# A fused decoder layer with top-k cross-attention: two row normalisations and a residual add change engines, and two stages change the order of their instructions

## The reference

```python
x = x + attn(layernorm(x))        # 4 branches x 16 heads, RMS norm and rope on q, banded masks, null values
x = x + xattn(layernorm(x), ctx)  # 16 heads; softmax over the 32 largest of 722 scores, times the values
x = x + ffn(layernorm(x))         # fft, a sparse complex weight, inverse fft: one real 512 x 512 matrix

def layernorm(x): return (x - mean(x)) / sqrt(var(x) + 1e-5)      # over the last axis
```

## Time and profile before

| | us |
|---|---|
| median of three runs | 2447.41 (2444.17 to 2450.51) |
| the profiled execution's own time | 2448.53 |
| its span | 2446.7 |

### The profile page before, as it was taken

One profiled execution on the slowest core, in us unless ns is written; L12 is line 12 of the kernel. 1 busy time (PEld: TensorE's weight loads), 2 busy tenths in 40 slices (PEclk: granted clock), 3 DMA queues, 4 the chain that ended last, 5 costly groups with the idle time before them and its releaser, 6 DMA issues. The chain is left out here.

```text
span 2446.7 us, 54297 instructions
## 1 busy us (share of the span) xinstructions
PE 2122.6 (87%) x19760; PEld 1650.1 (67%) x19760; DVE 1977.5 (81%) x3663; ACT 1265.8 (52%) x2464; POOL 1285.2 (53%) x1473
## 2 busy tenths in 40 slices
PE   2898999989897378999999999999899899899966
PEld 1565555656563267877778778778778788788754
DVE  4666565666642149999999999999999999999995
ACT  3232323223221147666666666676676676676652
POOL 2564554636450336566456565565565565555542
PEclk9999998989888689999999999999999999999987
DMA  5000000000002610010001000100100010001000
GB/s 180 11 15 17 13 17 13 10 19 11 14 15 91 161 28 18 13 36 18 20 25 29 21 24 13 37 18 19 37 18 19 25 29 19 25 13 36 5 5 11
DMA packets 41485, 70.11 MB, mean 29 GB/s; under 512 B 4638, under 2 KB 21166, under 8 KB 41260
## 3 DMA queue, kind: packets, MB, share of 16 engines
q1 hardware_dynamic: 35868, 56.31, 7.6%
q0 software_dynamic: 3632, 7.58, 1.3%
q10 hardware_dynamic: 1760, 3.28, 0.5%
HBM read 60.54 MB, written 9.86 MB: 29 GB/s over the span
## 5 line engine op out<-in xcount | busy, mean ns | idle before, releaser
L1390 DVE MATCH_REPLACE8 ca_W<-ca_top,ca_W 128x722 f32<-128x722 f32 (+1 forms) x624 | 553.0, 892 | 0.0
L1378 DVE MAX8 ca_top<-ca_W 128x8 f32<-128x722 f32 (+1 forms) x624 | 536.7, 897 | 2.2
L997 POOL TENSOR_TENSOR ca_S<-ca_S,ca_W 128x722 f32<-128x722 f32 (+1 forms) x208 | 358.6, 1743 | 276.0 <-ACT ca_W L1253 276.0
L1368 DVE MAX8 ca_top<-ca_S 128x8 f32<-128x722 f32 (+1 forms) x208 | 179.0, 898 | 64.9 <-ACT ca_S L1270 49.3
L1275 ACT ACTIVATE ca_PT<-ca_pT 128x768 f32<-128x768 f32 (+1 forms) x208 | 163.6, 786 | 129.4 <-PE ca_pT L1128 129.4
L974 POOL TENSOR_TENSOR ca_KL<-ca_K,ca_KH 128x384 fp32r<-128x384 f32 (+1 forms) x128 | 122.6, 958 | 183.3 <-ACT ca_KH L1245 180.5
L1253 ACT ACTIVATE ca_W<-ca_W,ca_shift 128x722 f32<-128x722 f32 (+1 forms) x208 | 186.0, 894 | 61.8 <-DVE ca_W L1390 61.4
L1161 PE MATMUL ca_pO<-ca_PT,ca_V 128*32 128x56 f32 (+5 forms) x4608 | 217.0, 225 | 0.0
L88 PE MATMUL ca_pS<-ca_KH,ca_QH 128*128 128x362 f32 (+1 forms) x384 | 150.7, 393 | 70.7 <-ACT ca_S L1270 63.5
L1263 ACT ACTIVATE ca_S<-ca_S,ca_shift 128x722 f32<-128x722 f32 (+1 forms) x208 | 175.8, 891 | 65.3 <-POOL ca_shift L989 65.2
L362 POOL TENSOR_TENSOR sa_ss<-sa_ss,sa_minus_half 100x16 f32<-100x16 f32 x64 | 192.3, 3023 | 22.1 <-DVE sa_ss L520 22.1
(11 more groups left out here) (213 smaller groups left out, 5286.2 us busy)
## 6 DMA issues: line engine op xcount, KB each, us to landing
ca_raw<-in_ctxT SPq DMA_DIRECT2D x32, 384.0 KB, 4.0
ca_raw<-in_ctxT SPq DMA_DIRECT2D x32, 338.0 KB, 3.0
sa_xin<-in_x SPq DMA_DIRECT2D x16, 200.0 KB
sa_xres<-in_x SPq DMA_DIRECT2D x16, 200.0 KB
x_scratch<-sa_x SPq DMA_DIRECT2D x16, 200.0 KB
x_scratch<-y_scratch POOLq DMA_DIRECT2D x16, 200.0 KB, 13.7
ca_xin<-x_scratch SPq DMA_DIRECT2D x16, 200.0 KB
ca_x<-x_scratch SPq DMA_DIRECT2D x16, 200.0 KB
```

The source lines that it names most:

```text
L997: pool.tensor_tensor(S[k][rows, :], S[k][rows, :], W[r][rows, :], ALU.subtract).then_inc(p_ready, 1)
L1368: dve.max(top[r][rows, 0:8], S[slot(t)][rows, :]).then_inc(peaked, 1)
L1378: n_of[t.i] = order.mark(dve.max(top[r][rows, 8 * k:8 * k + 8], W[r][rows, :]))
L1390: ins = dve.match_replace(W[r][rows, :], eight, W[r][rows, :], REMOVED)
```

## The change

Four things change.

1. Cross-attention, normalisations: `(x - mean) * rstd` moves from VectorE to ScalarE as `Identity(x * rstd + center)`; GpSimd makes the column `center = -mean * rstd` by one more small instruction behind each power. The attention output is copied from PSUM to `xin` by ScalarE (step 2), and GpSimd, not VectorE, adds it to `x2` (step 3). The statistics of `x2` move from round 0 to round 2 of step 3, and GpSimd's scales for it from step 3 to step 4.
2. Cross-attention, the loop over pairs of bodies: bodies 1 to 14 are written out one behind the other with constant counts.
3. The no-ops of `settle` in the cross-attention go.
4. Self-attention, VectorE's order: `low(1)` goes ahead of the two adds; `rope(0)` goes behind the last `squares`; `rope(1)` goes ahead of the reciprocal; `normalised()` goes behind `rope(3)`.

```diff
+                if cur:
+                    low(1)
+                if prev:
                     dve.wait_ge(num_used, b.count(NL, 2 - NL))
                     order.mark(dve.tensor_tensor(rb[:, 0, :], rb[:, 0, :], rb[:, 1, :], ALU.add))
...
                 if cur:
-                    for g in range(1, QC // 4):
-                        low(g)
+                    low(2)
+                    low(3)
...
-                    rope(0)
                     biased(3)
                     squares(2)
                     squares(3)
+                    rope(0)
                 if far:
                     statistics()
+                if nxt:
+                    rope(1)
...
                     dve.reciprocal(rden[:, :], pq[:, 3, 0:T]).then_inc(rden_ready, 1)
                 if nxt:
-                    rope(1)
                     rope(2)
+                    rope(3)
                 if far:
                     normalised()
-                if nxt:
-                    rope(3)
...
-            with eng.Fori(0, (B - 2) // 2) as i:
-                body(At(1, i, 2), 1, tiles=True, prev=True, nxt=True)
-                body(At(2, i, 2), 0, tiles=True, prev=True, nxt=True)
+            for n in range(1, B - 1):
+                body(At(n), n % 2, tiles=True, prev=True, nxt=True)
...
+            def scales(done):
+                order.after(order.mark(pool.tensor_tensor(rstd[:, :], mv[:, 1:2], minus_half[:, :], ALU.pow)))
+                pool.tensor_scalar(center[:, :], mv[:, 0:1], rstd[:, :], -1.0, ALU.mult, ALU.mult).then_inc(done, 1)
...
                     if s == 0 and nxt:
                         pool.wait_ge(var1_ready, bn.count(1, 1))
-                        pool.tensor_tensor(rstd[:, :], mv[:, 1:2], minus_half[:, :], ALU.pow).then_inc(rstd1_ready, 1)
+                        scales(rstd1_ready)
                     if s == 3 and prev:
+                        pool.wait_ge(y_kept, b.count(1, 0))
+                        pool.wait_ge(xb_ready, b.count(1, 0))
+                        pool.tensor_tensor(x2[:, :], x2[:, :], xin[:, :], ALU.add).then_inc(x2_ready, 1)
+                    if s == 4 and prev:
                         pool.wait_ge(var2_ready, b.count(1, 0))
-                        pool.tensor_tensor(rstd[:, :], mv[:, 1:2], minus_half[:, :], ALU.pow).then_inc(rstd2_ready, 1)
-                    if s == 4 and prev:
+                        scales(rstd2_ready)
                         pool.wait_ge(xn2_ready, b.count(1, 0))
                         pool.tensor_tensor(x2[:, :], x2[:, :], bias_f[:, :], ALU.add).then_inc(x2f_ready, 1)
...
+                    if s == 4 and prev:
+                        act.wait_ge(rstd2_ready, b.count(1, 0))
+                        act.activation(xin[:, :], x2[:, :], ACT.Identity, bias=center[:, 0:1],
+                                       scale=rstd[:, 0:1]).then_inc(xn2_ready, 1)
                     for x in slices(s, 0, b, par, tiles, nxt):
                         keep(*x)
...
                     for x in cur:
                         exps(*x)
+                    if s == 0 and nxt:
+                        act.wait_ge(rstd1_ready, bn.count(1, 1))
+                        act.activation(xin[:, :], xin[:, :], ACT.Identity, bias=center[:, 0:1],
+                                       scale=rstd[:, 0:1]).then_inc(xn1_ready, 1)
                     for x in slices(s, 1, b, par, tiles, nxt):
                         keep(*x)
+                    if s == 2 and prev:
+                        act.wait_ge(x1T_mm, bn.count(1, 1) if nxt else b.count(1, 1) if tiles else b.count(1, 0))
+                        act.wait_ge(y_mm, b.count(1, 0))
+                        act.activation(xin[:, :], pX[0:T, :], ACT.Copy).then_inc(y_kept, 1)
...
-                        if k == 3 and s == 0 and nxt:
-                            dve.wait_ge(rstd1_ready, bn.count(1, 1))
-                            dve.tensor_scalar(xin[:, :], xin[:, :], mv[:, 0:1], rstd[:, :],
-                                              ALU.subtract, ALU.mult).then_inc(xn1_ready, 1)
...
-                        if k == 0 and s == 3 and prev:
-                            dve.wait_ge(y_mm, b.count(1, 0))
-                            dve.wait_ge(xb_ready, b.count(1, 0))
-                            dve.tensor_tensor(x2[:, :], pX[0:T, :], x2[:, :], ALU.add).then_inc(x2_ready, 1)
+                        if k == 2 and s == 3 and prev:
                             dve.wait_ge(x2_ready, b.count(1, 0))
                             row_stats(dve, order, x2[:, :], stats[:, :], mv[:, :], var2_ready)
-                        if k == 0 and s == 4 and prev:
-                            dve.wait_ge(x1T_mm, bn.count(1, 1) if nxt else b.count(1, 1) if tiles else b.count(1, 0))
-                            dve.wait_ge(rstd2_ready, b.count(1, 0))
-                            dve.tensor_scalar(xin[:, :], x2[:, :], mv[:, 0:1], rstd[:, :],
-                                              ALU.subtract, ALU.mult).then_inc(xn2_ready, 1)
```

More of the change, by code:

```diff
@@ L803, in cross_program @@
         xin, x2 = (sb(n, [T, D]) for n in ("xin", "x2"))
-        stats, mv, rstd = sb("stats", [T, 6]), sb("mv", [T, 2]), sb("rstd", [T, 1])
+        stats, mv = sb("stats", [T, 6]), sb("mv", [T, 2])
+        rstd, center = sb("rstd", [T, 1]), sb("center", [T, 1])
         xT, qT = sb("xT", [128, CC, T]), sb("qT", [128, CC, T])
@@ L832, in cross_program @@
             sem(n) for n in ("pt_mm", "pt_ready", "o_mm", "o_kept", "ot_ready"))
-        y_mm, x2_ready, x2f_ready, f_mm, out_ready = (sem(n) for n in ("y_mm", "x2_ready", "x2f_ready", "f_mm", "out_ready"))
+        y_mm, y_kept, x2_ready, x2f_ready, f_mm, out_ready = (
+            sem(n) for n in ("y_mm", "y_kept", "x2_ready", "x2f_ready", "f_mm", "out_ready"))
         SETUP = [(WqT[:, :, :], A["WqT"].rearrange("(c p) o -> p c o", p=128)),
@@ L926, in load_context @@
                     need(sp, ctx_lo, b.next().count(4, 2 * half + piece - 1))
-                    settle(sp)
                     src = A["ctxT"][bass.ds(i, 1), 256 * piece:256 * piece + 256, k0:k0 + kn]
@@ L987, in shifts @@
                 pool.wait_ge(peaked, tb.count(NT, t.i + 1))
-                settle(pool)
                 pool.tensor_scalar(shift[rows, r:r + 1], top[r][rows, 0:1], -SCALE, None,
@@ L1125, in weights_T @@
                 need(pe, pt_ready, tb.count(NT, t.i))
-                settle(pe)
                 for k in range(KC):
@@ L1366, in body @@
                         dve.wait_ge(s_ready, tb.count(NT, t.i + 1))
-                        settle(dve)
                         dve.max(top[r][rows, 0:8], S[slot(t)][rows, :]).then_inc(peaked, 1)
```

## The result

| | before | change |
|---|---|---|
| median of four runs, us | 2448.74 (2444.17 to 2450.51) | 2369.63 (2366.99 to 2371.59) |
| profiled execution, us | 2448.53 | 2371.59 |

The ratio is 0.9679, with a 95% interval of 0.9662 to 0.9696. The change is faster by 79 us. I had forecast 122, so the time is 44 us above my number and at the very end of my range, where rival 2 stood.

The account below looks back on a forecast made before the run. Self-attention was taken as bound by a chain through TensorE with two gaps per batch, cross-attention by VectorE. 70 + 39 + 15 - 2 = 122 us off 2448.5 gave 2326 us, range 2305 to 2370.

Parts of the forecast that it names:

- rival 2: Cross-attention: ScalarE's wait starves VectorE, from about 3 us of new TensorE stall per batch; 39 us return, 2365; chance 0.12.
- Self-attention, 70 us: Self-attention: the new VectorE order shortens TensorE's gaps and keeps its clock up; 37.4 us per batch instead of 42.47.
- Rival 1: Self-attention: the clock still falls, costing 1.5 to 2.9 us per batch, 2347 to 2367; chance 0.20.
- I take it as hidden, cost nothing: Cross-attention step 4: ScalarE's wait for GpSimd's row scales delays the key slices, TensorE waits about 2 us; no cost.
- 2.8 us are left: Cross-attention: TensorE's room per batch, its busy 89.2 us against the new VectorE batch of 92.0.
- about 3 us of new TensorE stall: Cross-attention: the stall per batch from which ScalarE's wait was to starve VectorE.
- VectorE's work, 39 us: Cross-attention: lines 1400, 1418 and 1411 leave VectorE, shortening the steady batches by 39 us.
- 2 of loss at the ends: Cross-attention fill and drain: new copies, add, column operation and hand-over lose 2 us together.
- Jump waits, 15.1 us: Cross-attention loop: VectorE's six "issue" waits at the jump back go with the loop, 15.1 us.
- Rival 4: Cross-attention: straight code stalls as the jump did, five waits of 2.5 us per batch, 175 us, 2501; chance 0.03.
- The new operations: Cross-attention: ScalarE's normalisations and copy take about 0.65 us each, GpSimd's add 1.29, its column operations 0.2 each.
- rival 3: Cross-attention: GpSimd's add stops VectorE, 1.29 us in each of fifteen batches, 19 us, 2345; chance 0.04.

Follow-up runs that it names:

- two mends: The change with ScalarE's step-4 normalisation of x2 behind the exponentials, 2323.5 us; or with GpSimd's scales at the end of step 3, 2324.28 us.
- the first mend: The change with ScalarE's normalisation of x2 moved behind the exponentials of step 4: 2323.5 us, ratio 0.9485.
- the added delay: The change with two idle GpSimd powers of about 0.57 us each ahead of the step-4 row scales: 2412.8 us, ratio 0.9857.
- the straight loop alone: The kernel before with only cross-attention bodies 1 to 14 written out, no-ops kept: 2427.12 us, ratio 0.9911.

## Why the prediction was right and wrong, by its own steps

- **Self-attention, 70 us: right, and by its steps.** Forecast 37.4 per batch, measured 37.2 to 37.4 in twelve of fourteen; waits of 0.2, 0.5 and 0.6 forecast, 0.17, 0.70 and 0.63 measured; `y` 3.6 forecast, 3.65 measured. Rival 1 happened in two batches at 1.7 us each. Putting `rope(1)` back took 52 us of the gain away; 17 stayed, and their source is open. That `low(1)`'s move was part of the reason was not so.
- **"I take it as hidden, cost nothing" of ScalarE's wait: this is the step that failed.** It cost 46 us, by two mends that each remove it. The order of events was as worked out (shifts, power, column, normalisation, `keep_weights_T`, scores, key slice, third projection), but two numbers were wrong. TensorE's stall, put at about 2 us, was 3.72. And the margin "2.8 us are left" compared VectorE's 92.0 with TensorE's *busy* time, 89.2. TensorE has small waits of its own, 3.41 us per batch, which stand in the change, with the first mend and with the added delay alike; with them it needs 91.6, and the margin is 0.6 (0.8 by the mended kernel's own waits). With 2.8 of room a stall of 3.72 would have cost 0.9 a batch; with 0.6 it cost 3.1. Rival 2's point of decision, "about 3 us of new TensorE stall", was wrong in the same way: 0.6 is enough. Its mechanism is what happened, and at 2365 its price was near. I gave it 0.12.
- **VectorE's work, 39 us: too high.** With the wait mended, its busy time per batch is 91.78, and it was 94.0 (1222.02 / 13): 2.2 us less, where I took 2.6 off. That makes some 33 us and not 39. Two runs say the same: from the first maximum to the end the kernel takes 1537.1 us with the straight loop alone and 1505.6 with the first mend, 31.5 less, and 2 of loss at the ends were forecast beside the 39.
- **Jump waits, 15.1 us: low.** The straight code gave 22 us in two different kernels (in the second the no-ops went with it). I counted VectorE's row and not TensorE's 19.3 us of "issue" at the same jumps. The steady batches gave 17.2, between the two rows; 5 us lie outside them and stay unexplained. Rival 4 did not happen. The Trainium skill (Runtime: NRT & Kernel Launch, Instruction fetch mechanics) says that instructions are prefetched in sequence and that a taken branch out of the fetched window stalls; this case agrees, with waits at the jumps and 0.7 us of them in straight code.
- **The new operations.** GpSimd's add took 1.274 (forecast 1.29). ScalarE's normalisation took 0.802 and 0.814, not 0.65: I had taken a Square without operand pointers for it. The Trainium skill (ScalarE: Activation LUTs, What ACT_TABLE_LOAD costs) gives 186 ns plus 0.833 per element and 93 for each pointer operand, an estimate of 799 for two pointers and 512 elements, and the trace agrees. ScalarE has time to spare, so this mattered only in the chain of step 4, by 0.16.
- **The add stops VectorE (rival 3): did not happen.** The 624 later maxima stay at 886/900/916 ns (882/896/915 before): the median rose by 4 ns, and their busy time by 0.7 us in all (536.7 to 537.4). What I said of the normalisation, that GpSimd holds it up, the trace of the kernel before bears out (last section). The sharing of a port that I weighed does not reach them; the Trainium skill (SBUF — State Buffer, SBUF: two separate sides) limits it to operations in a 2-port mode or with two SBUF inputs, which agrees with these rows.
- **The sum.** With the wait mended the kernel takes 2323.5, and 2326 was forecast: a good number, but in part by luck, from one term 6 too high and one 7 too low. What it forecast was a kernel with the normalisation four instructions later in ScalarE's queue.

## What to carry to other kernels

When work leaves the bounding engine, compare the new pace with the next engine's busy time **and those of its waits that are not for the bounding engine**, over one period; the busy time alone showed 2.8 us of room where 0.6 were. When an instruction that waits goes into an in-order queue, put it behind everything that others wait for, or compute its input a step earlier: the same operation cost 46 us at the head of ScalarE's step and nothing behind its exponentials. Price a TensorE wait at more than its length, since a slower clock can follow it.

The best kernel measured is the change with ScalarE's second normalisation behind the exponentials of step 4: 2323.5 us, 5.15% under the kernel before and 46 us under the change. Scales one step earlier do the same.

## What the runs showed of the hardware that I had not expected

- With 1.22 us more of TensorE wait went 2.44 us more of busy time for the same 785 instructions: the stretch at 1.2 GHz around the wait was longer, and a second one stood some 50 us ahead of it.
- A wait of 1.87 us before `turn(3)` left the clock at 1.00 through `y` in all fourteen batches, while one of 2.00 before `turn(1)` was followed by a `y` of 5.7. Whether the place or the 0.13 us decides was not tried and stays open; so does why two batches of the change, with shorter waits, had a slow `y`.
- At a jump back TensorE stood idle for 3.2 us and VectorE for 2.5, and writing the code out cost nothing that shows on either.
- VectorE's normalisation lasted 539 to 549 ns at its new place behind round 1 of step 4, where line 1418's, at the head of that step, had a mean of 794. What holds it up can be read from the kernel before. One of line 1400's long ones, and the GpSimd instructions that ran when it started:

```profile
1284.91 1.70 DVE L1400 TENSOR_SCALAR ca_xin<-ca_xin,ca_mv,ca_rstd 100x512 f32<-100x512 f32 x1
...
1282.75 3.58 POOL L982 TENSOR_TENSOR ca_cL<-ca_raw,ca_cH 128x768 fp32r<-128x768 f32 x2
```

GpSimd's second instruction ends at 1286.33 (1282.75 + 3.58), and the normalisation 0.28 later. So it is throughout: of the 32 normalisations of lines 1400 and 1418, seven started with no large GpSimd instruction running and took 536 to 547 ns; each of the other 25 started while one ran and ended 0.28 to 0.29 us after it, or in one case (3.785 us) after the next, which followed at once. The 16 of the run with the normalisation on VectorE behind round 1 start behind GpSimd's scales, with nothing running on GpSimd, and last 539 to 549. The maxima keep their 0.9 us beside the same GpSimd work.
